# One evacuation for four PSUM banks, and pieces of the next chunk moved into the first eight heads, in an attention and feed-forward layer on eight cores

## The reference

```python
# x: (4, 4096, 1024) f32; 16 heads of 64; 64 features a head
x = x + layernorm(attn(layernorm(x)))     # causal linear attention over chunks
x = x + layernorm(ffn(layernorm(x)))
# attn: qkv = x @ w_qkv.T; f(z) = (proj^2 / sqrt(32)) * exp(clip(proj * s1 - s0)) * w,
#       proj = (z / |z|) @ omega, for q and k
#       kv, ks = running sums of kf * v and kf over time
#       out = (qf @ kv) / max(qf @ ks, 1e-6); return out @ w_out.T
# ffn:  x as 64 rails of 16; y = x @ rail_maker (4 heads); z = y @ rail_up (x4 wide)
#       h = gelu(z) (16384 wide); return h @ w_cproj.T     # 16384 -> 1024
```

## Time and profile before

| | us |
|---|---|
| time before, median of two runs | 4259.29 (4249.52 to 4269.07) |
| the profiled execution, its own time | 4259.2 |
| its span on the slowest core (core 6) | 4257.6 |
| the cores' spans | 4204.7 to 4257.6 |
| mean granted TensorE clock, any core | 0.718 to 0.722 |

### The profile page before, as it was taken

How to read it: one execution, slowest core, us unless ns; L and a number is a source line. 1 busy time by engine, 2 the same in 40 slices (tenths; PEclk the granted TensorE clock), 3 DMA queues, 4 the chain that set the end, 5 groups by cost and what they waited for, 6 DMA issues and landing times.

```text
span 4257.6 us, 31055 instructions; the slowest of 8 cores (4204.7 to 4257.6 us)
## 1 busy us (share of the span) xinstructions
PE 2232.1 (52%) x10253; PEld 1007.1 (24%) x10368; DVE 932.0 (22%) x1718; ACT 943.1 (22%) x1313; POOL 51.4 (1%) x73
## 2 busy tenths in 40 slices
PE   0333334544544455444445666667762776666664
PEld 0212212322222232222221222222221222222222
DVE  0222222223323233332343011111005101011013
ACT  0222323333222322223202111111102211111111
POOL 1000000000000000000000000000000000000000
PEclk9666666656666566566556888888885887888887
DMA  8000000000000000000002222211123022222221
GB/s 167 5 6 10 5 10 0 1 0 0 1 0 1 0 1 0 1 0 1 1 7 40 40 40 40 34 28 27 32 40 79 1 40 40 40 40 40 40 40 40
DMA packets 55082, 99.60 MB, mean 23 GB/s; under 512 B 2368, under 2 KB 18880, under 8 KB 53824
## 3 DMA queue, kind: packets, MB, share of 16 engines
q0 software_dynamic: 44880, 80.82, 11.8%
q1 hardware_dynamic: 10048, 16.79, 1.2%
HBM read 170.03 MB, written 8.39 MB: 42 GB/s over the span
## 4 chain that ended last, share of the span: by engine, by line
PE 47%; DVE 20%; DMA 12%; ACT 11%; issue 7%; DVEq 2%; ACTq 1%; POOL 0%; SPq 0%; POOLq 0%
PE psB L805 23%; DMA wc<-wcT 8%; PE psA L396 6%; PE psA L767 4%; DVE oacc L825 4%; PE psA L429 3%; DMA xa_bf<-x_carry 2%; DVE railsM L528 2%; PE psB L601 1%; DVE pn_bf L346 1%; DVE f32s L319 1%; PE psA L272 1%; DVEq L83 1%; PE psA L339 1%; ACT xa_bf L325 1%
## 5 line engine op out<-in xcount | busy, mean ns | idle before, releaser
L805 PE MATMUL psB<-hsl,wc 128*128 128x512 bf16 x4004 | 1059.9, 402 | 566.3 <-DMA wc<-wcT 443.1
L805 PEld LDWEIGHTS psB<-hsl,wc 128*128 128x128 bf16 x4096 | 375.1, 101 | 1119.6 <-issue 803.5
L778 ACT ACTIVATE hsl<-psA 128x512 bf16<-128x512 f32 x512 | 305.7, 597 | 1372.1 <-PE psA L767 1367.9
L825 DVE TENSOR_TENSOR oacc<-oacc,psB 128x512 f32<-128x512 f32 x224 | 153.9, 687 | 1440.0 <-PE psB L805 1408.0
L396 PE MATMUL psA<-ln_bf,wqkv_bf 128*128 128x256 bf16 x1536 | 254.7, 345 | 82.0 <-DVEq L83 56.3
L266 PE MATMUL psA<-xa_bf,allones_bf 128*128 128x256 bf16 x256 | 59.7, 413 | 386.2 <-DMA xa_bf<-x_carry 223.2
L767 PE MATMUL psA<-ln,railsM 32*128 32x512 bf16 x512 | 211.1, 415 | 24.5 <-DVEq L83 13.8
L396 PEld LDWEIGHTS psA<-ln_bf,wqkv_bf 128*128 128x128 bf16 x1536 | 186.1, 124 | 146.1 <-issue 88.4
L262 ACT ACTIVATE sq_bf<-xa_bf 128x2048 bf16<-128x2048 bf16 x32 | 61.1, 1909 | 459.7 <-DVEq L83 287.0
L339 PE MATMUL psA<-qk_bf,omega_bf 64*64 64x256 bf16 x384 | 50.9, 413 | 211.9 <-DVEq L83 211.9
L429 PE MATMUL psA<-wqkv_bf,ln_bf 128*128 128x512 bf16 x489 | 145.1, 462 | 31.3 <-DVEq L83 17.0
(11 more groups left out here) (150 smaller groups left out, 2018.2 us busy)
## 6 DMA issues: line engine op xcount, KB each, us to landing
wc<-wcT POOLq DMA_DIRECT2D x32, 2048.0 KB, 18.0
x_sb<-x_own SPq DMA_DIRECT2D x8, 1024.0 KB, 22.8
y_out<-oacc SPq DMA_DIRECT2D x8, 1024.0 KB, 4.4
wqkv_bf<-wqkvT POOLq DMA_DIRECT2D x8, 768.0 KB, 47.7
xa_bf<-x_carry POOLq DMA_DIRECT2D x8, 512.0 KB, 7.6
wout_bf<-woutT POOLq DMA_DIRECT2D x8, 256.0 KB, 66.2
rut_bf<-rut POOLq DMA_DIRECT2D x4, 128.0 KB, 5.6
omega_bf<-omega POOLq DMA_DIRECT2D x2, 128.0 KB, 14.8
```

The source lines that it names most:

```text
L778: A_((lambda a, fcl=fcl, zsl=zsl, hb=hb: a.activation(hb[:, fcl * 512:(fcl + 1) * 512], psA[:, zsl * 512:(zsl + 1) * 512], AF.Gelu)), wait ...
L805: t.matmul(psB[:, ob * 512:(ob + 1) * 512], wcbufs[fcl // 8][:, (fcl % 8) * 1024 + obi * 128: (fcl % 8) * 1024 + (obi + 1) * 128], hb[:, f ...
L825: V_((lambda v, g=g, obg=obg, ob=ob: v.tensor_tensor(AP(oacc, (obg * 4 + ob) * 1024 + g * 512, [[8 * 1024, 128], [1, 512]]), AP(oacc, (obg ...
```

## The change

It has two parts. In stage B, the eight calls of pump in the head loop stand before heads 0 to 7 instead of before heads 0, 2, 4 to 14. In the feed-forward part, the four evacuations of a group become one instruction over all four banks (128x2048), and the first product of a group waits for it; the three other banks' first products have no wait of their own. The order of the first product's waits is now ScalarE, weights, VectorE.

```diff
             for hh in range(H):
-                if hh % 2 == 0:
+                if hh < 8:
                     pump()
@@
-            evac_dv = [P.snap("dv")] * 4
@@
                     for obg in range(2):
-                        dv_guard = list(evac_dv)
+                        dv_guard = P.snap("dv")
                         for fcl in range(16):
@@
                                 w = []
-                                if fcl == 0:
-                                    w = [("dv", dv_guard[ob])]
-                                    if ob == 0:
-                                        w += [("ac", h_done_for[i]),
-                                              ("dwc", max(wc_sem))]
+                                if fcl == 0 and ob == 0:
+                                    w = [("ac", h_done_for[i]),
+                                         ("dwc", max(wc_sem)),
+                                         ("dv", dv_guard)]
@@
-                        for ob in range(4):
-                            if grp == 0:
-                                V_((lambda v, g=g, obg=obg, ob=ob: v.tensor_copy(
-                                    AP(oacc, (obg * 4 + ob) * 1024 + g * 512,
-                                       [[8 * 1024, 128], [1, 512]]),
-                                    psB[:, ob * 512:(ob + 1) * 512])),
...
-                            evac_dv[ob] = P.snap("dv")
+                        if grp == 0:
+                            V_((lambda v, g=g, obg=obg: v.tensor_copy(
+                                AP(oacc, obg * 4096 + g * 512,
+                                   [[8 * 1024, 128], [1024, 4], [1, 512]]),
+                                AP(psB, 0, [[2048, 128], [512, 4], [1, 512]]))),
+                               waits=[("pe", pm), ("dout", P.snap("dout"))])
+                        else:
+                            V_((lambda v, g=g, obg=obg: v.tensor_tensor(
+                                AP(oacc, obg * 4096 + g * 512,
+                                   [[8 * 1024, 128], [1024, 4], [1, 512]]),
+                                AP(oacc, obg * 4096 + g * 512,
+                                   [[8 * 1024, 128], [1024, 4], [1, 512]]),
+                                AP(psB, 0, [[2048, 128], [512, 4], [1, 512]]),
+                                op=ALU.add)), waits=[("pe", pm)])
```

## The result

The changed kernel takes 4219.97 us in the median of 11 executions, the kernel before 4264.44 us in the median of 10. The ratio of the changed kernel to the kernel before is 0.990, with a 95% interval of 0.988 to 0.992. That is 1.0% or some 43 us less, where 61 us less had been forecast. In ten more executions of the same kernel (after_again), compared anew with the kernel before, the ratio came to 0.996 (0.991 to 1.000), so the gain may be smaller than the first interval says.

The account below looks back on a forecast made before the run. Attention was taken as bound by a chain of waits, feed-forward by TensorE's products and its waits for weights and VectorE. 4259.2 - 33.6 (feed-forward) - 27.4 (attention passes) = 4198 us, range 4155 to 4240.

Parts of the forecast that it names:

- signs of being wrong: Evacuation over 2.7 us, slow stretches at nearly all stops or none, second passes of 5.7 us, transfers longer by earlier start.
- The stop: Feed-forward: one evacuation of 2.29 us shortens each of 48 stops by 0.36 us, 17.3 us in all.
- I leave the number of slow stretches at 26: Feed-forward: 26 of 48 stops still cost a slow stretch, some 1.5 us each, as before the change.
- The rival that every stop becomes slow: Feed-forward: the unbroken gap costs a slow stretch at all stops, 33 us more, 4231 us; chance 0.13.
- The loads: Feed-forward: at 14 stops the weight load is issued 1.02 us earlier, gaining 14.3 us.
- The rival gave the right size (no gain): Weight loads land when they did, held by memory eight cores share; 14.3 us lost, 4212 us; chance 0.10.
- The passes: Attention: second passes q1 and k1 take 3.65 us, 3.91 us gained in each of seven chunks, 27.4 us.
- cover and warm heads cancel: Attention: covering head tails is worth nothing either way, and four heads are warm in either order; no gain or loss.
- six of ten after an empty gap: Stage A alone: six of ten second passes after 2.57 us idle take 3.65 us, four 5.1 to 5.3.
- The rival on the slower side: Feed-forward: the gap leaves the clock low for 6.0 us, as a weight wait does; 4303 us; chance 0.03.
- the ends of the halves: Feed-forward: the final layer norm starts behind the last evacuation, 1.02 us earlier in each of two halves, 2.0 us.

Follow-up runs that it names:

- filler: The changed kernel with ten added 128x512 products into spare PSUM behind each group that has no load behind it; ratio to the kernel before 0.974.
- load_late: The changed kernel with one added VectorE instruction between evacuation and weight load at the 14 load places, loads issued about 1.1 us later; ratio to the kernel before 0.996.
- load_pe: The changed kernel with weight loads waiting for the group's last product instead of the evacuation; ratio to the kernel before 0.987, from two executions.
- pairs_apart: The kernel before with pump calls ahead of heads 0, 1, 2, 4, 5, 6, 8 and 9, two heads still between paired passes; ratio to it 1.000.

## Why the prediction was right in range, and where it was off

The measured 43 us less lie within the range, and the mechanisms of the stop and of the passes were those of the text, but two terms were too large. Their misses point the same way, and it is the width of the range (85 us) that holds them: that the time lies in it doesn't show the sum right. Of the prediction's own signs of being wrong one came true, transfers longer by what they start earlier, and another in part: 250 of 384 stops are slow, 88% of those behind a group with rails, where about half had been expected.

- **The stop.** 0.36 us a stop was forecast and 0.37 measured, the instruction at 2.29 and the return at 2.47 us. Right. The step that failed was "I leave the number of slow stretches at 26". Over eight cores it went from 188 to 250 of 384, 7.75 more a core, and took back some 10 of 18 us. The rival that every stop becomes slow was right in its direction and went too far: stops ahead of a group with rails' products didn't change (37 to 32), those behind one went from 61% to 88%. The prediction gave no reason for an unchanged number. The Trainium skill, "TensorE: Matmul & The Clock Gate", section "A second HAM failure mode: psum-queue depth-cycling", describes a clock that swings where TensorE pauses between groups of products. The traces agree with it, in the kernel before as in the changed one, and filler shows that the pause is the cause.
- **The loads.** 14.3 us were forecast, 0.4 measured in the profiled execution, and 6.6 lost in after_again. The issue came 1.03 us earlier, as forecast, and the transfer starts 2496.14 - 2491.56 = 4.58 us behind the evacuation's start. The step that failed was to keep the transfer's 27 us fixed. The rival gave the right size (no gain) with a mechanism that fell: load_late and load_pe show that issue time counts. What makes the transfers vary by more than the term itself is open.
- **The passes.** 27.4 us forecast, 23.7 measured in the start of the feed-forward part. The second passes take 3.65 us, as forecast, and TensorE waits 0.35 us for ScalarE ahead of them, 0.1 more than taken. A chunk is 3.4 us shorter and not 3.9; the wait explains 0.2 of the difference, and the rest was not traced. That cover and warm heads cancel agrees with pairs_apart, which changes the order and not the time. The evidence for fast second passes was thinner than it looked: six of ten after an empty gap is what core 6 had, and over the eight cores it is 24 of 80. That all 112 passes behind a head are fast was not to be had from those rows; here the guess that a gap with products in it does better was right.
- **The rival on the slower side** (a low clock for as long as behind a load) did not occur: slow groups without rails are some 1.5 us longer, as before, and those with rails 1.4 to 3.0 us, before 1.5 to 4.3.

On the mean core 61.0 us were forecast and 34.6 came: the loads account for 13.9 of the difference, the slow stretches for 9.9, the passes for 3.7; the stop itself and the ends of the halves gave some 1 us more than forecast.

## What to carry to other kernels

A stop of TensorE costs its length and, behind it, often a stretch at half clock if the stop was empty: in the changed kernel behind 88% of the stops after a group with rails and 29% of those before one, and behind none once the stops were filled. Shortening a stop by taking the work out of it can give back half of what it saves. Ordering the products so that one bank is finished, and evacuated, while the next is being filled removes the stop: worth 5% here, against 0.3 to 1% for a faster evacuation. Where two dense bursts depend on one another, let less light work stand between them: behind one attention head the second burst found the clock up in 112 of 112 cases, behind two in none.

## What the runs showed of the hardware that was not expected

- Added work made the kernel faster: ten useless products in each of the 48 stops without a load brought 1.6% against the changed kernel, over two thirds of it by removing all slow stretches; three placed right behind the group removed those behind groups with rails almost wholly (210 to 12 of 240), and none of those before one (32 and 33 of 112).
- The 4 MB of weights of a group (in the kernel's 16-bit form) take 26.0 to 27.7 us from issue to first product on the mean of the cores, by kernel, and 23.1 to 32.5 us by core and load.
- Sixteen products of 128x512 into one PSUM bank, while VectorE reads the bank next to it, run at 3.45 us, 0.216 each: as fast as the products of a fast group in the changed kernel, (14.26 - 0.2) / 64 = 0.22 us each.
